# A cross-attention chain on one Trainium2 core: written orders of all five engines replaced, fixed PSUM banks, a fourth group slot, and a residual transpose in 64-row tiles

## What is computed

```
# layer 0
q, k, v = x @ Wq, ctx @ Wk, ctx @ Wv            # 16 heads of 64
p = softmax(q k^T / 8 + col_bias)
x = (p v) @ Wo + bo + x
# layers 1, 2, 3
xn = x * rsqrt(mean(x*x) + eps) * norm_w
q, k, v = xn @ wq, ctx @ wk, ctx @ wv           # 16 query heads of 8, 4 kv heads
x = x + (softmax(q k^T / sqrt(8)) v) @ wo
```

## Time and profile before

| | us |
|---|---|
| median of 3 runs | 1381.1 (1379.0 to 1381.84) |
| span of the profiled execution | 1376.3 |
| PE busy in it | 1362.7 |
| DVE, ACT, POOL busy | 1064.6, 1003.3, 734.9 |

### The profile page before, as it was taken

One profiled execution on the slowest core, in us unless ns is written; L12 is line 12 of the kernel. 1 busy time (PEld: TensorE's weight loads), 2 busy tenths in 40 slices (PEclk: granted clock), 3 DMA queues, 4 the chain that ended last, 5 costly groups with the idle time before them and its releaser, 6 DMA issues.

```text
span 1376.3 us, 59054 instructions
## 1 busy us (share of the span) xinstructions
PE 1362.7 (99%) x25494; PEld 1055.6 (77%) x25494; DVE 1064.6 (77%) x2258; ACT 1003.3 (73%) x2207; POOL 734.9 (53%) x851
## 2 busy tenths in 40 slices
PE   9999999999999999999999999999999999999997
PEld 7777777777777777777787777777777777777875
DVE  4487777987778977778777788777798777778776
ACT  4667777767778677777677786777776777767886
POOL 5355456654456545466554565544665445655553
PEclk9999999999999999999999999999999999999999
DMA  5010010000000010100001001001011010010000
GB/s 151 18 30 22 15 34 16 26 27 23 26 23 22 27 27 23 28 18 26 26 24 26 23 22 27 27 24 28 17 27 27 23 27 25 19 36 22 7 23 14
DMA packets 46003, 37.02 MB, mean 27 GB/s; under 512 B 17072, under 2 KB 41520, under 8 KB 45744
## 3 DMA queue, kind: packets, MB, share of 16 engines
q1 hardware_dynamic: 44576, 32.89, 8.8%
q10 hardware_dynamic: 1168, 0.36, 0.1%
HBM read 16.42 MB, written 4.19 MB: 15 GB/s over the span
## 4 chain that ended last, share of the span: by engine, by line
PE 95%; ACT 2%; DVE 2%; issue 0%; POOL 0%; DMA 0%; SPq 0%; POOLq 0%
PE psum L954 18%; PE psum L942 16%; PE psum L1009 10%; PE psum L1027 8%; PE psum L969 8%; PE psum L991 7%; PE psum L1055 7%; PE psum L1019 5%; PE psum L980 5%; PE psum L1063 4%; PE psum L1032 3%; PE psum L961 2%; PE psum L1038 2%; ACT E L1141 1%; ACT E L1136 1%; DVE st L1226 1%
## 5 line engine op out<-in xcount | busy, mean ns | idle before, releaser
L892 POOL TENSOR_TENSOR E<-E,st 128x512 f32<-128x512 f32 x488 | 497.3, 1044 | 168.1 <-DVE st L1238 159.4
L1136 ACT ACTIVATE E<-E,inv 128x512 f32<-128x512 f32 x384 | 273.4, 722 | 135.8 <-DVE E L1230 134.3
L1226 DVE TENSOR_REDUCE st<-psum 128x8 f32<-128x512 f32 x372 | 240.4, 673 | 145.5 <-PE psum L991 145.1
L1235 DVE TENSOR_REDUCE st<-E 128x8 f32<-128x512 f32 x488 | 321.2, 665 | 35.3 <-ACT E L1129 28.2
L1141 ACT COPY E<-psum 128x512 f32<-128x512 f32 x512 | 275.1, 609 | 33.7 <-PE psum L1009 33.5
L954 PE MATMUL psum<-wv,cT 128*128 128x374 f32 (+1 forms) x768 | 273.3, 486 | 0.3 <-issue 0.3
L1230 DVE TENSOR_TENSOR E<-psum,st 128x512 f32<-128x512 f32 x372 | 248.3, 677 | 0.3
L904 POOL TENSOR_TENSOR nt<-nt,powers 128x2 f32<-128x2 f32 (+1 forms) x102 | 19.9, 196 | 420.0 <-DVE nt L1265 400.2
L942 PE MATMUL psum<-cT,wk 128*128 128x256 f32 x1024 | 240.5, 383 | 0.2 <-DMA cT<-in_ctx_t 0.2
L942 PEld LDWEIGHTS psum<-cT,wk 128*128 128x128 f32 x1024 | 191.5, 190 | 34.8 <-issue 1.5
L954 PEld LDWEIGHTS psum<-wv,cT 128*128 128x128 f32 x768 | 138.2, 189 | 73.5 <-ACT V L1097 8.5
(11 more groups left out here) (68 smaller groups left out, 1632.2 us busy)
## 6 DMA issues: line engine op xcount, KB each, us to landing
KB<-K SPq DMA_DIRECT2D x1536, 8.0 KB
cT<-in_ctx_t SPq DMA_DIRECT2D x32, 256.0 KB, 2.8
xq<-in_x_t SPq DMA_DIRECT2D x32, 128.0 KB, 2.1
out<-xT SPq DMA_DIRECT2D x30, 128.0 KB, 1.8
wk<-in_L_xattn_Wk SPq DMA_DIRECT2D x3, 256.0 KB, 5.8
wv<-in_L_xattn_Wv SPq DMA_DIRECT2D x2, 374.0 KB, 8.6
wq<-in_L_xattn_Wq SPq DMA_DIRECT2D x1, 512.0 KB, 7.7
wo<-in_L_xattn_Wo SPq DMA_DIRECT2D x1, 512.0 KB, 4.4
```

The lines of the kernel that those rows point to most:

```text
L892: e.tensor_tensor(E3, E3, wide(stat[s][u][:, 16:24]), ALU.mult).then_inc(g_nrm.sem, 1)
L1136: e.activation(E[s][u][:, :], E[s][u][:, :], ACT.Exp, scale=inv[s][:, u // 2:u // 2 + 1]).then_inc(a_exp.sem, 1)
L1226: e.tensor_reduce(stat[s][u][:, 0:8].rearrange("p (r h) -> p r h", r=2), scores_of[g, l, u], AX, ALU.max).then_inc(d_max.sem, 1)
L1235: e.tensor_reduce(stat[s][u][:, 8:16], heads(E[s][u][:, :]), AX, ALU.add).then_inc(d_sum.sem, 1)
```

## The change

The numbers of all tables are new, so that every engine has a new order, and so is `PERIOD` (whose value only shifts the groups' numbers against each other before sorting). `NS` is 4. The banks are a table, `PE_BANKS` with `BANK_ENDS`, one digit for each bank of a step, instead of a rule. A `t` step of a normal group is now two steps of 16 transposes with waits of their own, which stand apart or together. `x2` is four transposes of 64 rows and 128 columns into two banks instead of two of 128x128 into one, and ACT squares from both banks in one instruction. `k`, `v`, `q0` and the rest have the same instructions as before. The SBUF tiles of a fourth slot are the only new memory.

```diff
-NS = 3
+NS = 4
-PERIOD = 42.042923
+PERIOD = 41.572189
 PE_TIME = {
-    "t": {0: (-348.90236,), 1: (-317.45557,), 2: (-285.56016,), 3: (-253.49293,)},
+    "t": {0: (58.48538, 57.98938), 1: (94.03073, 94.57974), 2: (131.50574, 132.29199), 3: (153.23157, 161.39111)},
...
+PE_BANKS = {
+    "s": {0: ("57", "14"), 1: ("1245",), 2: ("0145",), 3: ("2345",)},
+    "x2": {1: ("12",), 2: ("67",), 3: ("45",)},
...
+def banks_of(kind, g, l, u):
+
+    return [int(i) for i in BANK_ENDS.get(g, PE_BANKS)[kind][l][u]]
...
-            if st[0] == "s" and l > 0:
-                at = min(([i, i + 1, j, j + 1] for i in range(5) for j in range(i + 2, 7)),
-                         key=lambda four: max(free[i] for i in four))
-            else:
-                at = sorted(sorted(range(8), key=lambda i: free[i])[:len(evictors)])
+            evictors, at = held_until(st), banks_of(*st)
+            assert len(at) == len(set(at)) == len(evictors)
...
                 elif kind == "t":
-                    for n, p in enumerate(halves(g, u)):
-                        emptied(w, before[st][2 * n] + before[st][2 * n + 1])
...
+                        w.wait_ge(g_nrm, ("nrm", g, l, 2 * u), ("nrm", g, l, 2 * u + 1))
+                    for r in range(2):
+                        for k in range(4):
+                            for i in range(2):
+                                rows, c = slice(64 * i, 64 * i + 64), 256 * r + 64 * k
+                                m = e.transpose(psum[:, at[i], c:c + 64],
+                                                E[s][2 * u + r][rows, 128 * k:128 * k + 128], ident[rows, rows])
...
                     for p in halves(g, u):
-                        m = e.transpose(bank[:, 128 * p:128 * p + 128], xT[s][:, 128 * p:128 * p + 128], ident[:, :])
+                        for i in range(2):
+                            rows = slice(64 * i, 64 * i + 64)
+                            m = e.transpose(psum[:, at[i], 64 * p:64 * p + 64], xT[s][rows, 128 * p:128 * p + 128],
+                                            ident[rows, rows])
...
-                        e.activation(QT[s][:, 2, tokens], bank[:, tokens], ACT.Square).then_inc(a_ev.sem, 1)
+                        e.activation(sq, x, ACT.Square).then_inc(a_ev.sem, 1)
```

More of the change, by code:

```diff
@@ L73 @@
+    "pv0": {0: (67.27841, 66.33441)},
+    "x2": {1: (78.29343,), 2: (112.64810,), 3: (141.56769,)},
+    "q": {1: (79.66104,), 2: (111.57745,), 3: (140.26477,)},
+    "pv": {1: (99.47708,), 2: (135.95306,), 3: (165.64905,)},
 }
 DVE_TIME = {
[L75 to L93, removed]
+    "add": {0: (49.47241, 51.25943, 47.56641, 48.87741)},
+    "max": {0: (50.66342, 52.45044, 48.28140, 50.06741),
+            1: (81.24307, 83.62909, 81.83908, 82.43509),
+            2: (113.39911, 114.59113, 115.78513, 113.99512),
+            3: (143.60364, 144.19965, 147.18573, 145.39368)},
@@ L138 @@
-    2: {
[L139 to L150, removed]
+        "k": {0: (48.72346, 45.16612, 46.99679, 50.45012)},
@@ L481 @@
+        "sum": {0: (46.69189, 46.69232, 63.68884, 65.70685)},
+        "rcp": {0: (59.57587, 58.38885, 65.59784, 66.41586)},
+        "wo0": {0: (76.29153, 78.39587)},
+        "sub": {1: (83.35223, None, 85.14224, None),
[5 rows of a table added]
     },
     31: {
-        "add": {0: (-119.87716, -119.6699, -122.49044, -123.16987)},
-        "max": {0: (-119.35079, -119.23138, -120.59121, -121.33631),
-                1: (-90.25966, -85.18078, -82.13575, -82.10246),
-                2: (-62.48423, -60.91201, -60.57903, -60.36904),
-                3: (-30.27588, -29.96241, -21.41472, -17.13109)},
@@ L498 @@
-        "sub": {1: (-90.24559, None, -81.0966), 2: (-61.3638, None, -60.0284), 3: (-29.3924, None, -16.06436)},
[3 rows of a table removed]
+        "add": {0: (46.13933, 44.87306, 46.73433, 45.54433)},
+        "max": {0: (49.11736, 47.92534, 48.52135, 47.32933),
+                1: (73.58617, 74.89915, 75.88121, 76.76329),
+                2: (88.74223, 90.13829, 91.55669, 92.19164),
+                3: (101.38341, 102.01836, 103.21239, 103.80840)},
+        "sum": {0: (53.13609, 55.41112, 53.73210, 51.03108)},
+        "rcp": {0: (54.32811, 56.20714, 54.44112, 51.74010)},
@@ L502 @@
+        "wo0": {0: (69.35924, 65.81883)},
+        "sub": {1: (74.30113, None, 77.35924, None),
[5 rows of a table added]
     },
```

917 lines of the change are left out of this document (499 added, 418 removed), and 102 rows, old and new, of tables (BANK_ENDS, DVE_ENDS, PE_ENDS).

## The result

The changed kernel takes 1383.4 us (median of 10 runs, 1380.3 to 1387.3), the kernel before on the same chip 1380.7 (10 runs). The ratio is 1.002, 95% interval 1.001 to 1.0029: 2.7 us slower where 3.7 us faster was forecast. The spans of the two profiled executions are 1379.7 and 1376.3 us. In each of the 10 runs of the changed kernel the time is 1.8 to 1.9 us above the span, and so it is in the later runs of the kernel before. So the 4.8 us of "Time and profile before" do not all lie around the program: some 3 us of them mean that the profiled execution of before ran faster than the median. The forecast difference is untouched by it, since both sides had the same 4.8.

A forecast was written before the change was run, and what follows sets the result against it. PE was taken as the bound, busy 1362.7 of 1376.3 us. Span 1376.3 - 4.1 (own steps) + 1.1 (waits) - 0.7 (pauses) = 1372.6, plus 4.8 gives 1377.4 us, 0.27% faster; range 1371.5 to 1386.5.

The forecast's parts named there:

- I take 0.05 us a group for 22 groups: PE's waits in the middle groups: 1.1 us in all, bounds 0 and 0.4 a group (9 us).
- The chain of layer 3: From scores of layer 3 to their `t`: work summing to 11.0 us must fit a distance of 10.9.
- The chain of layer 0: Work feeding layer 0's `t`: 19.8 us against 19.9 of PE steps, leaving 0.1 of cover.
- The two banks of `x2`: I take nothing: Scores after `x2` need banks ACT must empty: fits by under 0.1 us; 0.1 a group, 2 us, kept for the range.
- The saving of 0.28 on `x2`: Three `x2` a group, each beside a `t`, save 0.095 us each; 9.1 us in all.
- the 41.57 forecast: Period of an undisturbed middle group in us: 41.85 less 0.28, if nothing waits.
- the chains bind: Rival, slower: feeding chains 2% longer make two waits of 0.4 us a group, 8.8 us, giving 1385; chance 0.18.
- `x2` and the forms: PE's own steps: `x2` saves 9.1 us, extra stretches and changes of form cost 5.0; sum falls 4.1 us.
- The fourth slot: Group slots (`NS` = 4): no middle step was late for want of one, so no price.
- The end: taken as unchanged: Last groups: 8.5 us of PE idle in the last 119 us stays, 3 us either way.
- The pauses: Pauses inside PE's long dense stretches: 0.7 us less, between 3.9 less and 2 more.
- The sign that was named for it: If chains bind: period 41.9 us and over, PE idle ahead of `t` put down to POOL's `nrm`.

The follow-up runs named there:

- experiment 1: Kernel after with units 1 and 3 of layer 3 swapped in the order of `sum`, `rcp` (DVE) and `nrm` (POOL); 1379.7 us.
- experiment 5: Kernel after with new layer 3 `nrm` order, new banks for `wo`, `k`, `q0`, layer 3's `x2` earlier, layer 1's `q` copy earlier; 1376.3 us, ratio 0.9968 to kernel before.
- experiment 4: Kernel after with `x2` of layer 3 placed ahead of both halves of `t`; 1383.4 us.
- experiments 7 to 9: Kernel before with `x2` by rows in groups 4 to 23, 1393.9 us; that with layer 2's `x2` beside a `t`, 1394.4; kernel after with whole `x2`, 1409.5.
- experiment 2: Kernel after with other PSUM banks for `wo`, `k` and `q0` in groups 5 to 24; 1382.2 us.
- a shift of 212: Kernel with all four edits, with 1 blank matmul of 128 columns and 60 of 16 ahead, moving PE's instructions 212 places later; 1408.1 us.
- these shifts: Kernel with all four edits, PE's instructions moved 28 or 212 places later by blank matmuls ahead of the first step; 1384.8 and 1408.1 us.
- experiment 3: Kernel after with both the new `nrm` order of layer 3 and the new banks of `wo`, `k` and `q0`; 1381.9 us.

## Why the prediction was wrong, point by point

- **The failing step is "I take 0.05 us a group for 22 groups" for the waits of PE in the middle.** The chain of layer 3 had been added up as 11.0 us against a distance of 10.9, over by 0.1, and yet priced at half of that. It measured 0.16 a group (experiment 1). The chain was added up rightly: it takes 11.00 us in the kernel after. The distance was not: PE's bare steps take 10.77 (experiment 5), so the overrun is 0.23, of which 0.16 shows at the `t` and 0.06 is spent ahead of it on the bank of `wo`. The chain of layer 0, 19.8 against 19.9, makes nothing wait: the `pv` ahead of its `t` takes 1.03 us in all of 21 groups.
- **"The two banks of `x2`: I take nothing"** fell too: 0.05 a group (experiment 4), about half of the 0.1 that I had kept for it. Two of its numbers were off: the record of `x2` ends 0.29 us after its start, not 0.2, and PE reaches the scores in 0.72 us without the wait, not 0.77. The Trainium skill's warning (TensorEngine Tiling (Array Packing), Restrictions and Gotchas) that row tiling raises the pressure on PSUM fits in direction, but no run here separates the second bank from the first. And the bank of `wo`, 0.06 a group, was in no term: the table of banks was read for `x2` alone.
- Together the waits came to 6.2 us instead of 1.1. The saving of 0.28 on `x2` less 0.29 of waits gives the old 41.85 by chance, not by a common bound: with the waits gone it is 41.54, near the 41.57 forecast. The rival "the chains bind" named this mechanism; it had put 0.4 and 1385 on it. It is nearer to the measured 1383.4 than the forecast is, but for two chains 2% too long, where one chain, two banks and a copy made the waits.
- **`x2` and the forms were right.** PE's own steps fell by 4.6 us against 4.1; `x2` beside `t` takes 0.13 against 0.125; experiments 7 to 9 bear out the change of form in and out. The fourth slot was worth 0 in the old order, as said.
- **"The end: taken as unchanged"** was wrong by 3.45 us, beyond the 3 allowed. One pause of 1.05 us at 1225 is part of it. The rest are waits such as these, from PE's timeline after:

```profile
1332.99 0.71 PE L1095 MATMUL psum<-ident,E 64*128 64x64 f32 x16 [0.67 <-POOL E L981]
...
1338.39 0.65 PE L1138 MATMUL psum<-E,ones 128*32 128x64 f32 x32 [0.52 <-ACT E L1230]
...
1340.98 0.46 PE L1152 MATMUL psum<-QT,wos 128*128 128x128 f32 x2 [0.59 <-DVE QT L1343]
```

  They are read from the trace only. No experiment changed the end, and why its new order waits longer is open.
- **The pauses** were rightly taken as nearly unchanged in the middle (-0.9 against -0.7), for a poor reason: nearly all need a dense stretch, as I wrote, but also a place in PE's stream.
- The chance of slower, 0.20, was too low. A sum that exceeds its cover is a wait, and should have been the forecast. The sign that was named for it, idle time ahead of `t` put down to POOL, was all but hidden too.

## What to carry to other kernels

An order packed until no slack is left can turn a saving into waits, here by chance of the same size: add up, for every step, the chain that feeds it and the bank it writes, and price the overrun in full. Waits under one chain do not add (experiment 2), so relieve the last one first. Such waits hide mostly in overlapping records: read distances between starts, not idle time.

## What the runs showed of the hardware

**PE waits for its own instructions.** In dense small tiles it runs the 256 instructions of a packet in 2.1 to 3.2 us (ahead of 52 of the 55 pauses), and then may stand 0.3 to 1.9 us at a place 191 or 192 past a multiple of 256. Such pauses hold 1.3 to 7.3 us of idle time between 127 and 1300 us in the 14 traces. The Trainium skill (Trainium Architecture — The Big Picture, The software stack) has the streams copied to the engines when the program is loaded. That cannot be the whole of it here, since 202 packets arrive all through the run.

**A blank matmul of 16 columns cost as much as one of 128.** PE's timeline with a shift of 212, 0.21 us a record, against 0.22 with 128 columns ahead of the first step; it is why these shifts cost 3 and 22 us:

```profile
1.64 25.62 PE L1017 MATMUL psum<-E 128*128 128x16 f32 x120
```

**The clock can fall in the last waits.** Stretches of experiment 3 (length, PE busy, granted clock, DMA):

```profile
1300.00:1360.00 60.00, 54.20 (x1612) 1.00 0.06 16
1360.00:1370.00 10.00, 9.25 (x53) 0.59 0.01 2
1370.00:1380.00 10.00, 7.33 (x175) 0.90 0.13 41
```

PE was idle for a tenth of the 60 us ahead, then a part of its work ran at the lower level of 1.2 GHz; the eight extra matmuls (`FILLS`) at 1367.13 us took 3.78 us, where the kernel after took 1.99. In the profiled executions of the kernel after and of experiment 5, with like waits, the clock stayed at 1.00 up to 1370 us. What decides between the two is open.

It bears on the result. Of the 10 runs of the changed kernel six had a mean granted clock of 0.996 to 0.999 and a median of 1383.5 us, and four had 1.000 and 1382.0 us; the kernel before had 1.000 in 40 of the 41 runs in which it was run beside the experiments. So a part of the 2.7 us, by these medians about half, may be clock and not order. That is an estimate from four runs, and no experiment was made on it.
